# W2 split during the attention iterations and kept in HBM, and the bias of the first expert layer copied a step ahead

## The reference

```python
x = x + rbf_attention(layernorm(x))          # exp of exp(-dist), one head
x = x + cross_attention(ctx, layernorm(x))   # 16 heads, masked softmax
xs = layernorm(x)                            # 2048 tokens of 256
weights, sel = top_k(xs @ Wg, 2); weights = softmax(weights)
h = relu(xs @ W1[e] + b1[e])                 # 256 -> 1024, per expert
out_e = h @ W2[e] + b2[e]                    # 1024 -> 256
x = x + sum over the two chosen experts of weight * out_e
```

## Time and profile before

| | |
|---|---|
| median of 3 runs | 673.15 us (670.8 to 676.01) |
| the profiled execution | 675.28 us, of which the profile's span is 672.3 us |
| TensorE busy | 604.3 us, 90% of the span |
| VectorE busy | 407.6 us, 61% |
| ScalarE busy | 281.2 us, 42% |
| GpSimd busy | 213.3 us, 32% |
| moved by DMA | 85.34 MB |
| mean granted TensorE clock | 0.949 of full speed |

### The profile page before, as it was taken

How to read it: one execution, slowest core, us unless ns; L and a number is a source line. 1 busy time by engine, 2 the same in 40 slices (tenths; PEclk the granted TensorE clock), 3 DMA queues, 4 the chain that set the end, 5 groups by cost and what they waited for, 6 DMA issues and landing times.

```text
span 672.3 us, 15234 instructions
## 1 busy us (share of the span) xinstructions
PE 604.3 (90%) x4857; PEld 556.9 (83%) x4900; DVE 407.6 (61%) x994; ACT 281.2 (42%) x701; POOL 213.3 (32%) x262
## 2 busy tenths in 40 slices
PE   4766999999999999989858868999799999999992
PEld 4765888888898988877746868999799999999992
DVE  3536857777686767666894666676444444444441
ACT  4332374745545473625162732232343433344340
POOL 8311120512112020101062213432464545555531
PEclk9889999999999999998887978899799999999996
DMA  7382909080633619091256935365667676776741
GB/s 213 94 101 85 102 11 100 3 136 10 77 68 49 96 21 122 4 120 40 62 163 224 368 120 159 94 210 160 165 169 220 174 219 176 215 185 206 202 115 20
DMA packets 55430, 85.34 MB, mean 127 GB/s; under 512 B 6416, under 2 KB 44144, under 8 KB 55376
## 3 DMA queue, kind: packets, MB, share of 16 engines
q1 hardware_dynamic: 46368, 73.59, 45.3%
q0 software_dynamic: 7616, 10.26, 8.7%
q10 hardware_dynamic: 1392, 0.79, 0.4%
HBM read 62.44 MB, written 9.31 MB: 107 GB/s over the span
## 4 chain that ended last, share of the span: by engine, by line
PE 67%; DVE 12%; DMA 8%; issue 4%; ACT 4%; SPq 2%; DVEq 2%; POOL 1%; POOLq 0%
PE bank L1997 15%; PE bank L977 13%; PE bank L2041 13%; PE bank L1217 5%; PE bank L1274 4%; PE bank L1303 4%; DMA experts_w<-L_ffn_W 4%; PE bank L1271 3%; PE bank L1214 3%; DMA q_stack<-cq_lo 2%; ACT hid L2007 2%; PE bank L943 2%; DVE xn_ffn L896 1%; DMA exp_ring<-L_attn_Wo 1%; PE bank L1113 1%
## 5 line engine op out<-in xcount | busy, mean ns | idle before, releaser
L1997 PE MATMUL bank<-slots_t,w_now 128*128 128x128 f32 x1248 | 150.0, 280 | 3.1 <-DMA w_now<-L_ffn_W 3.1
L1997 PEld LDWEIGHTS bank<-slots_t,w_now 128*128 128x128 f32 x1248 | 146.8, 197 | 3.3 <-DMA w_now<-L_ffn_W 3.3
L2007 ACT ACTIVATE hid<-bank,b_tile 128x128 f32<-128x128 f32 x312 | 85.7, 376 | 124.1 <-DVE b_tile L2013 100.3
L1956 POOL DMA_INDIRECT out<-y,scatter_now x39 | 63.0, 1615 | 133.1 <-DVE y L2055 125.9
L1225 DVE TENSOR_REDUCE row_max<-bank 128x2 f32<-128x512 f32 x128 | 81.1, 683 | 13.0 <-PE bank L1217 13.0
L2041 PE MATMUL bank<-experts_w,hid_hi 128*128 x624 | 85.8, 291 | 0.5 <-issue 0.5
L1286 ACT ACTIVATE exp_ring<-bank 128x512 f32<-128x512 f32 x128 | 68.2, 608 | 36.8 <-PE bank L1274 36.8
L2018 DVE CAST hid_hi<-hid 128x512 fp32r<-128x512 f32 x78 | 33.6, 431 | 77.7 <-ACT hid L2007 59.7
L2041 PEld LDWEIGHTS bank<-experts_w,hid_hi 128*128 128x128 f32 x624 | 78.7, 194 | 0.6 <-issue 0.6
L1217 PE MATMUL bank<-k_stack,q_stack 96*128 96x256 f32 x256 | 68.0, 380 | 4.3 <-DMA q_stack<-cq_lo 4.3
L1274 PE MATMUL bank<-q_stack,k_stack 98*128 98x256 f32 x256 | 68.5, 388 | 0.0
(11 more groups left out here) (270 smaller groups left out, 1051.7 us busy)
## 6 DMA issues: line engine op xcount, KB each, us to landing
w_now<-L_ffn_W SPq DMA_DIRECT2D x39, 1024.0 KB
experts_w<-L_ffn_W SPq DMA_DIRECT2D x8, 1024.0 KB
k_stack<-ck_hi SPq DMA_DIRECT2D x32, 128.0 KB, 4.7
q_stack<-cq_hi SPq DMA_DIRECT2D x32, 128.0 KB, 6.7
ctx_in<-ctx SPq DMA_DIRECT2D x8, 256.0 KB, 7.7
k_stack<-ck_lo SPq DMA_DIRECT2D x16, 128.0 KB, 4.9
q_stack<-cq_lo SPq DMA_DIRECT2D x16, 128.0 KB, 8.1
out<-x SPq DMA_DIRECT2D x7, 256.0 KB, 7.7
```

The costliest lines, as they stand in the source:

```text
L1956: core.rows_out.at(eng.indirect_dma_start(core.out_rows, bass.IndirectOffsetOnAxis(ap=core.scatter_now[b.p][:, :], axis=0), core.y[b.p][:, ...
L1997: mm = eng.matmul(banks[half][:, f * P:(f + 1) * P], core.w1_now[b.p][:, c, start:start + P], core.slots_t[b.p][:, c, :], start=c == 0, st ...
L2007: act = eng.activation(core.hid[:, g, :], banks[half][:, f * P:(f + 1) * P], ACT.Relu, bias=core.b1_tile[b.p][:, g:g + 1])
```

## The change

- **Split.** Iterations 0 to 7 each take one expert, 7 first and 0 last. ScalarE issues the 1 MB load into the last place (`split_load`), behind a wait for the previous store. In four pieces (`split_piece`, 128 x 512), ScalarE rounds and VectorE subtracts: piece 0 between `st_moments` and `st_normalise` for cross-attention, piece 1 ahead of `st_transpose("xcT")`, piece 2 ahead of `st_normalise` 0, piece 3 behind exp 15 and ahead of `st_normalise` 2. GpSimd has no part in it any more.
- **Store and load.** Iterations 0 to 6 store both parts, 2 MB, to a new HBM tensor `w2_parts` from ScalarE's queue behind the k projection (`split_store`). Expert 0 stays in its place. SyncE loads 1 and 2, and behind `memory_over` 3, 2 MB each, in iteration 8 ahead of the rows of `b1` and `b2`; ScalarE issues the loads of 4 to 7 in iteration 9 behind `st_transpose("hT")`. The splits and the `W2` loads of `experts_rest_sync` and of the expert steps are gone.
- **Waits of TensorE.** `ex_out` waits for three loads, or for all seven where the tile's expert is one of the last four; from tile 6 on for all.
- **Expert tiles.** VectorE copies `b1_tile` a step earlier (`ex_bias`); ScalarE makes `hid_hi`, each half behind its own four `Relu`s. Number registers of written-out tiles are kept (`known`).

The new `split_*` functions and the places where the order changes:

```diff
+def split_load(core, eng, x):
+    n = NE - 1 - x
+    if n > 0:
+        eng.wait_ge(core.w2["out"], 16 * n)
+    loads(core, eng, split_part(core, 1).bitcast(F32).rearrange("p (k n) -> p k n", k=FT),
+          core.t["L0_ffn_W2"][x].rearrange("(k p) n -> p k n", p=P), core.w2["in"])
+def split_piece(core, name, eng, x, piece):
+    n = NE - 1 - x
+    hi, lo = split_part(core, 0, piece), split_part(core, 1, piece)
+    if name == "scalar":
+        if piece == 0:
+            eng.wait_ge(core.w2["in"], 16 * (n + 1))
+        eng.activation(hi, lo.bitcast(F32), ACT.Copy).then_inc(core.w2["hi"], 1)
+    elif name == "vector":
+        eng.wait_ge(core.w2["hi"], PIECES * n + piece + 1)
+        eng.tensor_tensor(lo, lo.bitcast(F32), hi.bitcast(F32), ALU.subtract).then_inc(core.w2["lo"], 1)
+def split_store(core, eng, x):
+    eng.wait_ge(core.w2["lo"], PIECES * (NE - x))
+    loads(core, eng, core.w2_dram[x], core.experts_w[:, (NE - 1) * PLACE:].bitcast(F32), core.w2["out"])
@@ attention
     at(-1, st_moments, 0)
+    if name == "scalar" and it.v < NE:
+        split_load(core, eng, NE - 1 - it.v)
...
-    if placing and name in ("scalar", "gpsimd"):
-        split_expert(core, name, eng, 1)
...
     at(0, st_moments, 1)
     exps(2, 8, 9)
-    if placing and name in ("scalar", "gpsimd"):
-        split_expert(core, name, eng, 2)
+    split(0)
     at(0, st_normalise, 1)
...
     exps(2, 11)
+    split(1)
     at(0, st_transpose, "xcT")
...
     exps(2, 12)
+    split(2)
...
     exps(2, 13, 14, 15)
+    split(3)
     at(3, st_normalise, 2)
...
     at(-1, st_project, "k")
+    if name == "scalar" and it.v < NE - 1:
+        split_store(core, eng, NE - 1 - it.v)
...
     at(2, st_transpose, "hT")
-    if it.v == 2 and name in ("scalar", "gpsimd"):
-        split_expert(core, name, eng, 0)
+    if placing and name == "scalar":
+        eng.wait_ge(core.w2["parts"], 16 * (EARLY - 1))
+        for x in range(EARLY, NE):
+            load_expert(core, eng, x)
@@ experts_sync
     core.e["av"].wait(e, LAST_BATCH.back(1), 3)
-    for x in range(EARLY, POOL_SPLITS):
+    e.wait_ge(core.w2["out"], 16 * (NE - 1))
+    for x in range(1, EARLY - 1):
         load_expert(core, e, x)
     memory_over(core, e)
+    load_expert(core, e, EARLY - 1)
@@ load_expert
+    place = core.experts_w[:, (NE - 1 - x) * PLACE:(NE - x) * PLACE]
+    loads(core, eng, place.bitcast(F32), core.w2_dram[x], core.w2["parts"])
@@ experts
     elif name == "vector":
+        at(1, ex_bias)
@@ ex_hidden, scalar, after each half's four Relus
+            if half == 0:
+                core.m["out"].wait(eng, b.back(2))
+            core.m["h"].wait(eng, b, half)
+            part = slice(half * half_tiles, (half + 1) * half_tiles)
+            core.m["hid_hi"].at(eng.activation(core.hid_hi[b.p][:, part, :], core.hid[:, part, :], ACT.Copy))
```

More of the change, by code:

```diff
@@ L47 @@
 PLACE = 2 * FT * D
-EARLY = 1
-POOL_SPLITS = 3
+EARLY = 4
+PIECES = 4
 QROWS = 2 * 3 * HD
@@ L470, in make_events @@
               "vec pool both filler filled prefix counted delta ex slots table tabled idx b1_in b1_t order".split()}
-    core.w2_in = [sem(core, f"w2_in{i}") for i in range(2)]
-    core.w2 = {n: sem(core, "w2_" + n) for n in "hi lo lo_pool".split()}
+    core.w2 = {n: sem(core, "w2_" + n) for n in "in hi lo out parts".split()}
     core.w1_in = dma_event(core, "w1_in")
@@ L729, in exps, with split @@
             at(lag, st_exps, n)
+    def split(piece):
+        if it.v < NE:
+            split_piece(core, name, eng, NE - 1 - it.v, piece)
     if name == "sync":
-        if it.v == 1:
-            for x in range(EARLY):
-                load_expert(core, eng, x)
         if it.v >= 0:
@@ L1431, in experts_rest_sync @@
     ex_load(core, "sync", e, Step(0, 1))
-    core.e["p_hT"].wait(e, LAST_BATCH)
-    for x in range(POOL_SPLITS, NE - 1):
-        load_expert(core, e, x)
 def load_expert(core, eng, x):
[L1439 to L1446, removed]
@@ L1458, in split_expert, with split_part @@
+def split_part(core, part, piece=None):
+    start = (NE - 1) * PLACE + part * FT * D
+    if piece is None:
+        return core.experts_w[:, start:start + FT * D]
+    width = FT * D // PIECES
+    return core.experts_w[:, start + piece * width:start + (piece + 1) * width]
+def split_piece(core, name, eng, x, piece):
+    n = NE - 1 - x
+    hi, lo = split_part(core, 0, piece), split_part(core, 1, piece)
     if name == "scalar":
-        loaded(core, eng, x)
+        if piece == 0:
+            eng.wait_ge(core.w2["in"], 16 * (n + 1))
@@ L1916, in expert_of, with tile_number @@
 def expert_of(core, eng, b):
+    if isinstance(b.v, int) and (eng, b.v) in core.known:
+        return core.known[eng, b.v]
+    x = tile_number(core, eng, b)
+    if isinstance(b.v, int):
+        core.known[eng, b.v] = x
+    return x
+def tile_number(core, eng, b):
     return eng.value_load(core.tile_expert[0:1, bass.ds(b.v, 1)], min_val=0, max_val=NE - 1)
@@ L1983, in ex_load, with ex_bias @@
                                 rows[:, bass.ds(x * -1 + (NE - 1), 1), :, :]), b)
+def ex_bias(core, name, eng, b):
+    x = expert_of(core, eng, b)
+    core.m["h"].wait(eng, b.back(2))
+    core.m["b1t"].at(eng.tensor_copy(core.b1_tile[b.p][:, :], core.b1_cols[:, bass.ds(x * FT, FT)]))
 def ex_hidden(core, name, eng, b):
@@ L2009, in ex_hidden @@
             core.m["h"].at(act)
-    elif name == "vector":
-        x = expert_of(core, eng, b)
-        core.m["h"].wait(eng, b.back(2))
-        core.m["b1t"].at(eng.tensor_copy(core.b1_tile[b.p][:, :], core.b1_cols[:, bass.ds(x * FT, FT)]))
-        core.m["out"].wait(eng, b.back(2))
-        for half in range(2):
-            part = slice(half * half_tiles, (half + 1) * half_tiles)
-            core.m["h"].wait(eng, b, half)
-            core.m["hid_hi"].at(eng.tensor_copy(core.hid_hi[b.p][:, part, :], core.hid[:, part, :]))
+            if half == 0:
[3 more added lines that the diff above has]
+            core.m["hid_hi"].at(eng.activation(core.hid_hi[b.p][:, part, :], core.hid[:, part, :], ACT.Copy))
+    elif name == "vector":
         core.m["hid_hi"].wait(eng, b)
```

58 lines of the change are left out of this document (16 added, 42 removed).

## The result

The changed kernel takes **689.66 us** (median of 4 runs, 689.14 to 691.43) against 672.46 us for the kernel before on the same chip: a ratio of 1.0253, 95% interval 1.0207 to 1.0299. It is 17.2 us slower. The forecast was 684.4 in a range of 663 to 699. The direction was right and the size too small by a third. The parts of the sum were further off than the sum: two errors of opposite sign cancel in part, as the last part shows.

A forecast was written before the change was run, and what follows sets the result against it. TensorE's products were taken to bound the kernel, with holes in the turn from attention to experts. 11.0 + 2.3 + 5.3 - 7.4 = +11.2 us gave 684.4 us against the median 673.15, range 663 to 699.

The forecast's parts named there:

- Cost 1: Attention iterations: the rounding and subtracting pieces and the 1 MB load delay TensorE, 11.0 us in sum.
- TensorE's two waits: Iterations 2 to 6: TensorE idles 0.5 us ahead of the `xn_cross` transposes and 0.9 ahead of the k projection, 1.4 each.
- Iteration 1 at 3.5: Attention iteration 1: the 1 MB load and pieces put the normalise 1.8 us later, the bias add holds `xnT` 1.7 more.
- Cost 2: Attention: 2 MB stores beside the stacks cost 2.3 us in iteration 0 and are hidden in iterations 2 to 6.
- The rival far slower: Attention: stores go ahead of the stacks, costing 17 us instead of 2.3, time 699; chance 0.14.
- Gain 1: Turn to experts: without GpSimd's splits `xn_ffn` saves 8.4 us, of which 4.8 remain because `b1` lands late.
- Gain 2: Turn: splits of experts 3 to 7 go, but the normalised-row store queues behind four loads; first expert output 5.3 us later.
- Gain 3: Expert tiles: earlier `b1` and ScalarE rounding remove 2.10 us of `filler` wait, 2.8 of gather wait, plus 2.5 clock: 7.4.
- The estimate of 2.5 us for the clock: Expert tiles, within Gain 3: 2.5 us saved on products that would no longer follow waits and run at lowered clock.

## Why the forecast was right in direction and short in size

**Cost 1, 11.0.** The step from TensorE's two waits was right: 0.38 and 0.69 measured for 0.5 and 0.9, and 1.5 us per full iteration (39.3 less 37.8, without stores) for 1.4. The 0.4 between the waits' 1.07 and 1.5 lie in rows that count as busy. Iteration 1 at 3.5 was mis-sized: without stores it lost 0.7, and the 4.01 us that ScalarE waited there for the 1 MB load in the changed kernel did not set TensorE's time. (Without stores the load is on the chain there, but TensorE waits 1.63 us for `xn_cross`, against 1.56 before.) Measured to iteration 8: 5.5, or 7.5 without the 2.0 us wait that before's own trace has in iteration 0.

**Cost 2, 2.3.** This is the step that failed: 17.6 us measured (23.1 less 5.5), 13.7 with the shortest attention part of the four executions. The lateness of the stacks was about right. I had 2.3 us; the low part lands 2.5 us later by the median (10.6 for 8.1), and 1.9 in iteration 0 (9.69 for 7.82). That is luck in part: I had the store meet only the last 2.3 us of the stacks, and it met nearly the whole low part. Two things were missed. First, I read the slack of iterations 2 to 6 from one late iteration, gave it to iteration 2 as well, and had no term for iteration 1. Landing less wait shows when TensorE wanted the tile, counted from its issue: 9.69 - 3.14 = 6.6 us in iteration 0, 12.04 - 4.51 = 7.5 in iteration 1, 11.81 - 1.70 = 10.1 in iteration 2, and some 10.8 later. In 0 and 1 few `exps` and scores of earlier batches stand in between, and the rows of before say so: these iterations last 30 us, not 37.8. Second, I added no clock to a stall in attention, though I had added it in the turn. In the changed kernel it is 3.3 and 2.3 us behind the waits of 3.14 and 4.51, in the kernel with `b1` first nothing behind the first. The rival far slower had nearly the right sum, 17, with the wrong mechanism: in iterations 3 to 6 `q_stack` came not 4.2 us late but some 3 (11.14 for 8.1), and was hidden but for 0.3.

**Gain 1.** The 8.4 us of `xn_ffn` went, and `b1` took over, as forecast. It landed 16.64 us after its issue; the transpose gained 7.2 us on the attention's shift (23.1 less 15.9), not 4.8. SyncE's loads ahead of it were issued 1.4 us earlier than I had them (353.11 less 23.1 is 330.0, for 331.4); the other 1.0 is not worked out.

**Gain 2, minus 5.3.** The wait is there, VectorE idle 14.83 us ahead of the first `y` with the DMA as releaser. But against the attention's shift `y` came 1.0 us earlier (22.1 less 23.1), not 5.3 later, so the store landed some 6 us ahead of my reckoning. The bytes explain this. I had 14.1 MB ahead of its landing (my own terms add up to 13.75), with four `W1` tiles among them. Two of the four were issued from 371.34 on and waited for by nobody, and DMA had dropped from 426 GB/s (379 to 380) to 148 (382 to 383), when ScalarE's loads were just being issued (382.21): these two were through by then. From 382 to 414 only 11.6 MB moved (2 us at 197 GB/s, 24 at 410, 6 at 225), and the 2.1 MB of two tiles are 5.1 us at 410. SyncE's issues, and ScalarE's:

```profile
371.34 25.54 SPq L1991 DMA_DIRECT2D w_now<-L_ffn_W  x4
...
382.21 2.19 ACTq L484 DMA_DIRECT2D experts_w<-w_parts  x4
```

I had also assumed that `W1` tiles on SyncE's queue share the rate evenly with ScalarE's queue. Tile 2's was issued at 392.30 and landed at 409.49: 17.2 us, in which at 411 GB/s 7.1 MB moved, for its 1.05 MB. The Trainium skill (DMA: Bandwidth & Descriptors, Queues, rings and completion order) says engines go round between queues packet by packet; the forecast weighed this rule and put `y` at 393 by it, against 397.5. The trace agrees in so far as the queue with the smaller rows got much less than half; but that `y` is at 391.2 less the shift does not show it, since the bytes account for that. No run here varies the rows, so why tile 2 got so little stays open. With the stores issued first `y` came 12.5 us earlier and the time hardly moved, so the bytes are what counts.

**Gain 3, 7.4.** As a size it stands at 7.2 us alone. As terms it doesn't, so the match is luck: 2.8 were to come from the rows of tile 13, and every kernel with this part still waits 3.1 to 3.5 us for them. I had 2.1 for `filler`, and the two steps with the filler products gave 6.0, as ScalarE waited for the bias copy there. The estimate of 2.5 us for the clock was no half of 5.47 either, which is 2.7. In the changed kernel the gain shows from the rows of tile 4 to those of tile 7, where the shift falls from 21.0 to 14.9.

**The sum.** My forecast for attention was short by 9.8 (23.1 for 13.3), the turn was better by 5.6 (7.7 for 2.1), nearly all of it in gain 2, and the trace's 15.4 come out at the end; the medians have 17.2. That the total was only 6 us off is luck: the two errors cancel in part.

## What to carry to other kernels

Before you call a transfer hidden, read its slack in each iteration, the first ones above all, since a pipeline that is still filling has less work to hide it behind; and allow for a lowered clock behind a stall of TensorE, here anything from nothing to as much as the stall again. A store put beside small transfers that TensorE waits for costs what their delay costs; move it to where nothing else moves (675.84 us instead of 689.66). Where a stretch runs at full DMA rate, change its bytes, not its order. Where one engine's copy holds up another, look at what stands ahead of it in its queue: moving the bias copy and two subtractions, with the rounding given to ScalarE, took 14 us off the kernel before.

## What the runs showed of the hardware

- A 2.1 MB store alone lands in 6.3 us; beside the stacks in 10.9, and their low part lands in 10.6 instead of 8.1 (7.1 in the kernel without stores).
- Waits of 3.14 and 4.51 us were followed by mean granted clocks of 0.61 to 0.74 over 6 us windows, between the two levels (0.5 is 1.2 GHz, 1.00 is 2.4). In another execution a wait of 3.23 us was followed by 1.00.
- A 1 MB load on one queue took 17.2 us beside 2.1 MB loads on another, while 7.1 MB moved in all.
- Loads reached 410 GB/s at a DMA share of 0.99. The stretch of the stacks shows a share of 1.17 at 116 GB/s, and yet a store of 2.1 MB beside it delayed the stacks by 2.5 us in the median (10.6 for 8.1), where its bytes alone at 410 GB/s are 5.1.
- VectorE's `xn_ffn` took 9.20 us with GpSimd's subtractions beside it and 0.73 without them.
